# Two of the last batch's row scatters move ahead of its gate products, and TensorE's filler ahead of the experts becomes one run of 14

## The reference, cut to what matters

```python
x = x + layernorm(attention(layernorm(x)))
xf = layernorm(x)
scores = softmax(xf @ gate_w + gate_b);  top_vals, top_idx = top_k(scores, 2)
y  = sum over the 2 chosen e of top_vals * (silu(xf @ w1[e] + b1[e]) * (xf @ w3[e] + b3[e]) @ w2[e] + b2[e])
z  = silu(xf @ sw1 + sb1) * (xf @ sw3 + sb3) @ sw2 + sb2      # shared, inner width 352
out = x + layernorm(y + z)
```

## Time and profile before

| what | value |
|---|---|
| time of 3 runs | 1213.74, 1215.54, 1216.63 us; median 1215.54 |
| the profiled execution | 1213.77 us, of which 1211.3 us are the span from the first to the last instruction |
| busy in the span | PE 1068.8 us (88%), DVE 847.2 (70%), POOL 837.4 (69%), ACT 713.9 (59%) |
| mean granted clock of TensorE | 0.941 of full speed |
| the parts | batches to about 915 us, experts 921 to 1143 us, last part to 1211 us |

### The profile page before, as it was taken

How to read it: one execution, slowest core, us unless ns; L and a number is a source line. 1 busy time by engine, 2 the same in 40 slices (tenths; PEclk the granted TensorE clock), 3 DMA queues, 4 the chain that set the end, 5 groups by cost and what they waited for, 6 DMA issues and landing times.

```text
span 1211.3 us, 26878 instructions
## 1 busy us (share of the span) xinstructions
PE 1068.8 (88%) x8520; PEld 701.6 (58%) x8520; DVE 847.2 (70%) x2283; ACT 713.9 (59%) x1569; POOL 837.4 (69%) x984
## 2 busy tenths in 40 slices
PE   2389999999999999999999999999857999999800
PEld 1245565666656566565666656655435888888600
DVE  4378788787787877878778777775232666666586
ACT  0107677676676766767667676677512555555434
POOL 4535669788787887878778777566663666666667
PEclk9559999999999999999999999999978999999955
DMA  4333333313323133231332313323122444544276
GB/s 92 97 106 101 86 97 92 111 55 123 110 82 112 55 122 105 88 110 57 118 106 92 100 57 119 96 69 119 56 64 79 124 125 124 158 125 123 93 232 184
DMA packets 104681, 126.16 MB, mean 104 GB/s; under 512 B 17422, under 2 KB 85344, under 8 KB 99936
## 3 DMA queue, kind: packets, MB, share of 16 engines
q1 hardware_dynamic: 91638, 104.54, 29.0%
q0 software_dynamic: 8704, 18.11, 4.2%
q10 hardware_dynamic: 4202, 1.81, 0.5%
HBM read 78.06 MB, written 45.42 MB: 102 GB/s over the span
## 4 chain that ended last, share of the span: by engine, by line
PE 83%; DVE 6%; POOL 2%; issue 2%; ACT 1%; DMA 1%; SPq 0%; POOLq 0%; DVEq 0%; ACTq 0%
PE heads_ps L1474 13%; PE score L1464 12%; PE wide L1502 11%; PE wide L1624 7%; PE wide L1439 7%; PE wide L1504 5%; PE score L1452 3%; PE wide L1605 3%; PE wide L1606 3%; PE score L1596 3%; PE misc L1482 2%; PE wide L1535 2%; PE wide L1622 2%; DVE mx L1276 2%; DVE f_st L1081 1%
## 5 line engine op out<-in xcount | busy, mean ns | idle before, releaser
L1276 DVE TENSOR_REDUCE mx<-wide 128x2 f32<-128x1024 f32 (+3 forms) x384 | 390.8, 1042 | 104.6 <-PE wide L1504 103.0
L946 ACT ACTIVATE values<-score 128x512 f32<-128x512 f32 (+1 forms) x704 | 375.0, 557 | 128.5 <-PE score L1464 100.2
L833 POOL TENSOR_SCALAR_AFFINE_SELECT values<-values 128x512 f32<-128x512 f32 x256 | 162.0, 639 | 140.9 <-ACT values L946 138.5
L1502 PE MATMUL wide<-qk 72*128 72x512 bf16 (+3 forms) x1024 | 246.9, 307 | 4.4 <-DVE mx L1276 3.2
L1464 PE MATMUL score<-qk 75*128 75x512 bf16 (+3 forms) x1024 | 239.9, 301 | 2.4 <-ACT values L946 1.9
L878 POOL DMA_INDIRECT token_scratch<-spread,e_id x144 | 137.3, 954 | 95.8 <-issue 75.1
L1504 PE MATMUL wide<-maskneg,identb 128*128 128x128 bf16 x1024 | 200.1, 224 | 0.0
L1474 PE MATMUL heads_ps<-values 128*32 128x512 f32 (+3 forms) x2048 | 171.0, 440 | 0.0
L822 POOL DMA_INDIRECT sorted_scratch<-zr,places x128 | 128.7, 1006 | 43.0 <-issue 22.2
L1464 PEld LDWEIGHTS score<-qk 75*128 75x128 bf16 x1024 | 89.2, 99 | 98.4 <-ACT values L946 44.9
L1502 PEld LDWEIGHTS wide<-qk 72*128 72x128 bf16 x1024 | 101.8, 99 | 60.0 <-issue 13.0
(11 more groups left out here) (196 smaller groups left out, 1978.2 us busy)
## 6 DMA issues: line engine op xcount, KB each, us to landing
qk<-parts_scratch SPq DMA_DIRECT2D x192, 192.0 KB
parts_scratch<-spread SPq DMA_DIRECT2D x16, 768.0 KB
qk<-sorted_scratch SPq DMA_DIRECT2D x144, 66.0 KB
front<-token_scratch SPq DMA_DIRECT2D x16, 512.0 KB, 4.0
xt<-attn_x SPq DMA_DIRECT2D x16, 256.0 KB, 6.0
xr<-attn_x SPq DMA_DIRECT2D x16, 256.0 KB, 6.9
x_scratch<-z SPq DMA_DIRECT2D x16, 256.0 KB, 6.5
shared_scratch<-s_out SPq DMA_DIRECT2D x16, 256.0 KB, 6.2
```

The costliest lines, as they stand in the source:

```text
L833: nc.gpsimd.affine_select(out=prob[n][:, :, 0:P], in_=prob[n][:, :, 0:P], compare_op=ALU.is_ge, fill=0.0, base=0, pattern=[[0, HG], [1, P] ...
L946: nc.scalar.activation(free_ap(prob[kb][:, hs_[0], :], [[1, N * len(hs_)]]), score[SCORE_RING.buffer(b, step)][:, 0:N * len(hs_)], ACT.Exp ...
L1276: nc.vector.tensor_reduce(mx[:, h0:h0 + len(hs_), j:j + 1], src, axis=AX.X, op=ALU.max).then_inc(p1_max, 1)
L1502: nc.tensor.matmul(o, q4[e][0:ROWS, h, j * P:(j + 1) * P], k4[e][0:ROWS, h, 0:L], start=True, stop=False)
```

## The change

POOL's order for the last batch was d0 d1 d2 H1 H2 d3 d4 d5 d6 d7. It becomes d0 d1 d2 d3 d4 H1 d5 d6 d7 H2. Only POOL does `H` steps, so no other engine's order changes. PE's filler was 8 matmuls ahead of the wait for the first block and 8 behind it; it becomes 14 ahead of the wait and none behind it.

```diff
-FILL = 8
+FILL = 14
 DRAIN = (
-    "rstats U2 G2 d0@-1 d1@-1 d2@-1 rX rL choose rexp H1@-1 chosen G0@-1 U0@-1 D K@-1 counts@-1 H2@-1 place@-1 "
-    "blocks@-1 ends@-1 rows@-1 d3@-1 d4@-1 U1@-1 G1@-1 d5@-1 d6@-1 d7@-1 U2@-1 G2@-1 D@-1 "
+    "rstats U2 G2 d0@-1 d1@-1 d2@-1 rX rL choose rexp chosen G0@-1 U0@-1 D K@-1 counts@-1 place@-1 blocks@-1 "
+    "ends@-1 rows@-1 d3@-1 d4@-1 H1@-1 U1@-1 G1@-1 d5@-1 d6@-1 d7@-1 H2@-1 U2@-1 G2@-1 D@-1 "
 )
 ...
                 if k == 0:
                     pe.wait_ge(e_in[j], 16 * BG * (r + 1))
-                if isinstance(n, int) and n == 0:
-                    kept_busy(FILL)
                 if not (isinstance(n, int) and n < 2):
```

## The result

| | before | after |
|---|---|---|
| median of 20 runs | 1215.22 us (1213.32 to 1216.63) | 1212.09 us (1209.82 to 1214.12) |
| ratio | | 0.9973, 95% interval 0.9966 to 0.998 |
| the profiled execution, its span | 1213.77, 1211.3 | 1212.07, 1209.7 |

The change makes the kernel 3.1 us faster (medians), 3.0 were forecast. In a second measurement the medians were 2.5 us apart and the ratio was 0.9978 (0.9968 to 0.9988).

A forecast was written before the change was run, and what follows sets the result against it. Two paths to the first expert block were taken to bound the kernel, the scatters' the later. After: filler end 921.93 + first block 1.48 = 923.41 against 926.46, 3.0 us off 1215.54: 1212.5 us, range 1210.0 to 1215.2.

The forecast's parts named there:

- Path 1: Scatters on POOL, their landing, SP's loads: last scatter d7 issued 4.11 us earlier, first block in at 916.85 instead of 920.96.
- Path 2: H2, step D, ACT's copy, filler: D starts 3.39 us later, at 912.88; filler ends at 921.93, now the later path.
- ACT's copy and the filler: On PE behind step D: filler starts 0.73 us after D's end; 14 fillers take 2.96 us at full clock.
- D starts at half clock: Last batch's step D on PE: after 5.66 us idle it begins at 1.2 GHz, taking 5.36 us instead of 3.06.
- r: Time step D runs at half clock, losing r/2: taken as 4.6 us, with bounds 4.2 and 5.9.
- The formula: End of the first L1624 pair at 921.11 + r/2: gain 3.2 us with r = 4.2, 2.4 with 5.9.
- the first block: First expert block on PE, first transpose to end of first L1624 pair: 1.48 us at full clock instead of 2.08.
- A (the clock holds): Rival: clock stays full through PE's gap before step D; pair ends 5.3 us earlier, time 1210.2 us; 8%.
- B (D does not wake the clock): Rival: the clock's rise counts only from the filler behind step D; 0.2 us more than now, 1215.7 us; 12%.
- C (cold experts, slower): Rival: experts begin and stay at half clock; slower by 2.4 us if the rise comes at 928.5, 1218.0 us; 5%.
- D (something else holds the loads): Rival: tails or tables, not scatters, hold the first block, so SP's loads do not move; about 1214 us; 5%.

The follow-up runs named there:

- warm kernel without filler: Also written "warm, no filler": the changed kernel with 20 fillers ahead of the last batch's step D and none behind; 1259.79 us, before 1264.82 (ratio 0.9962).
- the change again: The changed kernel itself, measured a second time against the kernel before; 1212.71 us, before 1215.24 (ratio 0.9978).
- filler only: The kernel before with 14 fillers ahead of the first block's wait, none behind, and the old POOL order; 1262.63 us, before 1265.96 (ratio 0.9978).
- H2 after d5: The changed kernel with H2 between d5 and d6 instead of behind d7, the 14 fillers kept; 1259.68 us, before 1264.82 (ratio 0.9969).
- order only: The kernel before with the new POOL order and the old filler, 8 and 8; 1262.03 us, before 1265.96 (ratio 0.9970).

## Why the prediction was right

**Path 1.** Right. The distances from d0 came as worked out: the first of SP's loads was issued 13.05 us behind it instead of 17.06, so 4.0 us earlier, where 4.1 were forecast.

**Path 2 becomes the later one.** Right. D's first matmul came 12.50 us behind d0 (12.44 forecast) after 5.72 us of idle time (5.66), and ACT's copy and the filler 0.73 us behind D. The fillers ran at the full clock.

**D starts at half clock.** Right in kind; the size was the weakest term. The clock was at 0.50 from 914.3, 0.6 us before D, to 917.7:

```profile
914.30:914.40 0.10, 0.00 (x0) 0.00 (x0) 0.00 (x0) 0.00 (x0) 0.10 (x1) 0.51 0.05 0
914.40:917.60 3.20, 2.66 (x12) 2.60 (x13) 0.00 (x0) 0.00 (x0) 0.40 (x1) 0.50 0.18 43
917.60:917.80 0.20, 0.20 (x3) 0.20 (x2) 0.00 (x0) 0.00 (x0) 0.00 (x0) 0.72 0.73 188
917.80:930.00 12.20, 11.07 (x65) 7.31 (x64) 3.69 (x15) 4.25 (x15) 0.00 (x0) 1.00 0.38 98
```

That is r = 2.8 us, where I took 4.6 with bounds of 4.2 and 5.9. D took 4.37 us (914.94 to 919.31), not 5.36, so this term of the sum was 1.0 us too large. In the five profiles with the gap of 5.7 us D took 4.4, 4.5, 4.5, 4.7 and 5.6 us, so r lay between about 2.8 and 5: my lower bound was wrong. It came from three rises of one trace, and the one that gave the bound was no start at half clock: in the earlier trace rows the clock is still at 1.00 up to 902.0, with PE at work since 901.2, and was low for 3.4 us only (902.1 to 905.5). The page "TensorE: Matmul & The Clock Gate" of the Trainium skill (Part 1) says that the switch is not tied to when the kernel's work begins, and these five agree: the same gap and the same work gave lengths 1.2 us apart. In the same five profiles the clock fell 2.4 to 5.3 us after PE had stopped at the end of U2, where the prediction had 4.0 and 5.4.

**The formula.** With r = 4.6 the sum gave 3.05 us of gain in the stretch; it was 3.82. The pair was to end 20.67 + r/2 behind d0: 22.07 with r = 2.8, and it was 22.20. The 0.13 us left is the first block, 1.60 us instead of 1.48: at the full clock it waits 0.20 us for ACT's copy.

**The rivals.** A (the clock holds) did not occur in any profile with this gap. B (D does not wake the clock) is refuted by the rise at 917.7, inside D, and by the kernel without filler, whose first block ran at full clock directly behind D. C (cold experts, slower) did not occur with the change; its mechanism did in the warm kernel without filler, from another gap. D (something else holds the loads) fell with the loads' 4.0 us.

**Luck in the number, and what stays open.** The stretch says 3.7 to 3.8 us, the medians 3.1 and 2.5. That 3.1 came out beside the forecast 3.0 is in part luck: D's term was too large, and the medians show less than the traces. They mix two kinds of executions, which the mean granted clock of an execution tells apart. In the last sitting before took 1213.82 us (median) in its five executions at 0.940 to 0.941 and 1215.77 in its eleven at 0.934 to 0.936; the change took 1209.76 in three at 0.941 to 0.943 and 1213.16 in eight at 0.934 to 0.935 (one of each kernel lies between). So it gained 4.1 us in the first kind, to which the profiles of before and of the change again belong, and 2.6 in the second. Why less there is not shown. Before's profile had a late rise of the clock (5.0 us), and a shorter one would make before faster than its profile, but no execution of before of the second kind has a trace.

## What to carry to other kernels

When two paths meet, work out both after the change: here each half of the edit gave about what both together gave, and the next microseconds lay on the path that the change itself had made the later one. Count the filler as work: 14 matmuls on a path that ends last cost 3.0 us, and their place is in a wait (ahead of D, or behind it only as long as the loads take to land). A granted clock read off one execution at one gap is one sample; take its bounds wider than the samples.

## What the runs showed of the hardware that was not expected

The clock can fall after a gap in PE's work has ended, with PE at work again: behind 2.27 us of idle time (filler only) it fell 0.1 us into the matmuls, behind 2.06 us (warm, no filler) 0.7 us and behind 3.25 us (H2 after d5) 1.2 us into them. Before's trace already had a fall with PE at work, in the earlier trace rows at 902.0. It need not come: before's D ran at the full clock behind the same 2.27 us, and so did filler only's first blocks behind 3.12. Behind 1.40 to 1.41 us D took its full-clock 3.06 us in all five profiles with 20 fillers ahead of it.

The kernel before took 1215 us in the first measurement and in the last sitting, and 1265 us on the chip of the other two. There PE's weight loads for the up product stopped about once in four blocks, which before's own trace, taken on the chip of 1215, does not show in the experts (before has no trace on the slower chip). Who waited for whom on PEld, order only, 935 to 1180:

```profile
PEld wide L1624 <- issue: 34.9, 39, 1.2
```

What PE waited for there is not visible in the profile, and no run looked into it.
